# Scatters in batches of four that wait for landings, in place of waits on PE's progress

## What is computed

```python
x = x + (segment_sum(edge_weight * h[dst], src) @ weight + bias)
x = x + ((1 + eps) * h + segment_sum(relu(h[src] + edge_attr), dst))
x = x + L2(h)   # twice: segment_sum(w * x[c], r), w = dinv[r] * dinv[c], with self loops
x = x + L3(h)   # segment_sum(h[row] * norm, col), with self loops
```

## Time and profile before

| | us |
|---|---|
| median of 3 runs | 9,079.17 (9,056.56 to 9,087.81) |
| the profiled execution | 9,074.16 |
| its span | 9,072.3 |
| PE busy | 6,311.8 (70%) |
| DVE busy | 5,135.0 (57%) |
| ACT busy | 3,658.8 (40%) |
| POOL busy | 4,155.1 (46%) |
| POOL's scatters, 3,125 | 3,071.8, 983 ns each |

### The profile page before, as it was taken

One profiled execution on the slowest core, in us unless ns is written; L12 is line 12 of the kernel. 1 busy time (PEld: TensorE's weight loads), 2 busy tenths in 40 slices (PEclk: granted clock), 3 DMA queues, 4 the chain that ended last, 5 costly groups with the idle time before them and its releaser, 6 DMA issues.

```text
span 9072.3 us, 246452 instructions
## 1 busy us (share of the span) xinstructions
PE 6311.8 (70%) x98024; PEld 5439.8 (60%) x98025; DVE 5135.0 (57%) x7430; ACT 3658.8 (40%) x6626; POOL 4155.1 (46%) x4228
## 2 busy tenths in 40 slices
PE   5555555555555555555555555579999899999999
PEld 4444444444444444444444444468888899999999
DVE  5555555555555555555555555599999911111565
ACT  3444444444444444444444444478888600000000
POOL 2455555555555555555555555568888600000000
PEclk6677666676666667666666676799999999999999
DMA  6666566666666666666665666579999987888998
GB/s 172 186 180 179 177 181 183 183 187 179 190 183 181 177 179 200 182 177 181 191 185 177 185 190 184 162 251 316 316 318 316 306 272 261 283 276 277 283 266 213
DMA packets 1540180, 1969.31 MB, mean 217 GB/s; under 512 B 620045, under 2 KB 1204095, under 8 KB 1538767
## 3 DMA queue, kind: packets, MB, share of 16 engines
q1 hardware_dynamic: 1064800, 1272.38, 47.4%
q10 hardware_dynamic: 374342, 523.47, 18.5%
q0 software_dynamic: 100000, 158.60, 5.6%
HBM read 1335.36 MB, written 618.65 MB: 215 GB/s over the span
## 4 chain that ended last, share of the span: by engine, by line
PE 41%; another core or an unknown queue 17%; issue 13%; DVE 12%; ACT 10%; ACTq 2%; DMA 2%; POOL 2%; SPq 0%; DVEq 0%; POOLq 0%
PE pG L2347 9%; PE pT L2230 7%; PE pG L2374 7%; ACT stg L2585 5%; PE pT L2234 3%; PE pG L2186 3%; DVE doh L1724 2%; PE pT L2347 2%; ACT dfar L2552 2%; PE pR L2347 2%; DVE msum L1936 2%; PE pG L2197 2%; PE pG L2195 1%; PE pG L2311 1%
## 5 line engine op out<-in xcount | busy, mean ns | idle before, releaser
L1420 POOL DMA_INDIRECT recB<-rec,qpos x3125 | 3071.8, 983 | 2782.7 <-PE pT L2230 1376.0
L2230 PE MATMUL pT<-soh,doh 128*128 128x128 bf16 x10600 | 1820.9, 269 | 1608.3 <-ACT stg L2585 1317.4
L2585 ACT CAST stg<-pT 128x512 fp8e4<-128x512 f32 x2650 | 1497.7, 585 | 1977.5 <-PE pT L2230 1147.4
L2230 PEld LDWEIGHTS pT<-soh,doh 128*128 128x128 bf16 x10600 | 1042.5, 118 | 1867.8 <-ACT stg L2585 1421.5
L2234 PE MATMUL pT<-car,qidb 128*128 128x256 fp8e4 x2597 | 932.9, 359 | 32.5 <-issue 32.0
L1732 DVE TENSOR_REDUCE val<-pG 128x5 f32<-128x490 f32 x628 | 417.6, 665 | 878.7 <-PE pG L2197 385.4
L1737 DVE TENSOR_TENSOR rec<-pG,wN 128x480 f32<-128x480 f32 x314 | 206.6, 658 | 1173.2 <-remote 1053.1
L2311 PE MATMUL pG<-mpl,doh 128*128 128x144 bf16 x10388 | 765.9, 227 | 38.6 <-POOL mpl L1471 28.7
L1724 DVE TENSOR_TENSOR doh<-dm,pG 128x2560 bf16<-128x2560 bf16 x530 | 783.7, 1479 | 3.0 <-ACT dm L2671 2.6
L1724 DVE TENSOR_TENSOR doh<-smd,pG 128x2560 bf16<-128x2560 bf16 x530 | 783.4, 1478 | 0.0
L1724 DVE TENSOR_TENSOR soh<-smd,pG 128x1280 bf16<-128x1280 bf16 x530 | 432.5, 816 | 514.9 <-PE pT L2230 376.8
(11 more groups left out here) (265 smaller groups left out, 14180.2 us busy)
## 6 DMA issues: line engine op xcount, KB each, us to landing
recB<-zt ACTq DMA_DIRECT2D x102, 2425.5 KB
brec<-recB SPq DMA_DIRECT2D x477, 495.0 KB
erec<-recB SPq DMA_DIRECT2D x477, 495.0 KB, 5.5
cl<-cA SPq DMA_DIRECT2D x80, 2560.0 KB, 10.9
cA<-stg ACTq DMA_DIRECT2D x530, 320.0 KB
cl<-cA SPq DMA_DIRECT2D x40, 2720.0 KB, 11.2
drow<-dlD SPq DMA_DIRECT2D x157, 640.0 KB
srowB<-srD SPq DMA_DIRECT2D x265, 320.0 KB, 5.9
```

The lines of the kernel that those rows point to most:

```text
L1420: p.indirect_dma_start(recF, bass.IndirectOffsetOnAxis(ap=qpos[:, s, c:c + 1], axis=0), rec[:, s, c, :], None).then_inc(s_sc[s], 16)
L2230: ins = t.matmul(bank[:, h * 256 + b * 128:h * 256 + b * 128 + 128], doh[:, o, 2 * e + b, h * 128:(h + 1) * 128], soh[:, o, 2 * e + b, :], ...
L2585: a.copy(stg[:, o, :, e * 256:(e + 1) * 256], B8[6 + (g * 5 + e) % 2][:, :].rearrange("p (h x) -> p h x", h=2), saturate=False).then_inc(e ...
```

## The change

The waits of `paced` and `ranked` are left out. The 20 scatters of a slot are five batches of four, counted through over all slots (`batches`); batch B raises semaphore B % 3, in place of one semaphore for each s, and begins when batch B-2 has landed. The five scatters of slot (0, 2) are batch 0. `slot_free` and the wait of the first `load_bucket` of a chunk wait for the three last batches of the slot in question (`all_landed`). `hold` with a value that is known when the program is built no longer raises its counter; nearly all holds of the first stage are of that kind.

```diff
@@ -229,7 +229,10 @@
 
         def hold(eng, sem_, val):
 
-            eng.wait_ge(sem_, val).then_inc(s_hold, 1)
+            if isinstance(val, int):
+                eng.wait_ge(sem_, val)
+            else:
+                eng.wait_ge(sem_, val).then_inc(s_hold, 1)
 
         def cols(ap, i, g):
             return ap[:, bass.ds(i * TL + g * G, G)]
@@ -1334,14 +1337,29 @@
 
             return K * 16 + (16 if s == 2 else 0)
 
-        def scattered(K, s):
-            return K * (16 * SB) + (80 if s == 2 else 0)
+        BATCH = 4
+
+        def batch_done(B):
+
+            return s_sc[B % 3], (B // 3 + 1) * 16 * BATCH + (16 if B % 3 == 0 else 0)
+
+        def batches(K, s):
+
+            return 1 + (mcnt(K, s) - 1) * (SB // BATCH)
+
+        def all_landed(eng, K, s):
+
+            if mcnt(K, s) == 0:
+                hold(eng, *batch_done(0))
+                return
+            for B in range(batches(K, s) + 2, batches(K, s) + 5):
+                hold(eng, *batch_done(B))
 
         def slot_free(eng, K, s):
 
-            if isinstance(K, int) and scattered(K - 1, s) <= 0:
+            if mcnt(K - 1, s) < 0:
                 return
-            hold(eng, s_sc[s], scattered(K - 1, s))
+            all_landed(eng, K - 1, s)
 
         def reached(eng, sem_, val):
             if not isinstance(val, int) or val > 0:
@@ -1387,21 +1405,7 @@
             io(p.iota(mio[:, :, :, :], [[SB, 3], [1, SB], [0, 2]], base=0, channel_multiplier=0,
                       allow_small_or_imprecise_dtypes=True))
 
-            PACE = {0: {2: 4, 4: 6, 6: 8, 8: 10, 12: 12, 14: 14, 16: 15, 18: 16},
-                    1: {2: 4, 4: 7, 6: 9, 8: 10, 10: 13, 12: 14, 14: 15, 18: 18},
-                    2: {2: 8, 4: 10, 6: 13, 8: 14, 10: 15, 16: 16, 18: 19}}
-            RANKED = {0: {13: 2, 17: 3}, 1: {9: 1, 13: 3, 17: 4}, 2: {11: 1, 14: 2}}
-
-            def paced(K, s, c):
-
-                back, g = SUMMED[s][1]
-                hold(p, e_ca, ((K - back) * JG + g) * 5 + PACE[s][c])
-
-            def ranked(K, s, c):
-
-                hold(p, e_rk, (mcnt(K, s) + 1) * 4 + RANKED[s][c])
-
-            def scatter(K, s, first=False, pace=False, following=True):
+            def scatter(K, s, first=False):
                 n = mcnt(K, s)
                 hold(p, e_pos, n + 1)
                 hold(p, e_mu, n * 2 + 2)
@@ -1413,19 +1417,18 @@
                     for h in range(2):
                         hold(p, s_pz[h], K * 16)
                 for c in range(15 if first else 0, SB):
-                    if pace and c in PACE[s]:
-                        paced(K, s, c)
-                    if pace and following and c in RANKED[s]:
-                        ranked(K, s, c)
+                    B = 0 if first else batches(K, s) + c // BATCH
+                    if c % BATCH == 0 and B >= 2:
+                        p.wait_ge(*batch_done(B - 2))
                     p.indirect_dma_start(recF, bass.IndirectOffsetOnAxis(ap=qpos[:, s, c:c + 1], axis=0),
-                                         rec[:, s, c, :], None).then_inc(s_sc[s], 16)
+                                         rec[:, s, c, :], None).then_inc(batch_done(B)[0], 16)
 
             scatter(0, 2, True)
             for s in range(3):
                 scatter(1, s)
             for K in range(2, NK):
                 for s in range(3):
-                    scatter(K, s, pace=True, following=(K, s) != (NK - 1, 2))
+                    scatter(K, s)
             def aggregated(g):
 
                 p.wait_ge(e_ad, ((NK - 1) * JG + g) * 2 + 2)
@@ -2831,8 +2834,7 @@
             def load_bucket(K, g):
                 c = K * JG + g
                 if g == 0:
-                    for s in range(3):
-                        held(sp, s_sc[s], scattered(K, s))
+                    all_landed(sp, K, 2)
                 held(sp, e_ag, c - 4)
                 nb = nbk(g)
                 sp.dma_start(brec[:, g % 5, 0:nb, :], recB[bass.ds(K, 1), :, g * GB:g * GB + nb, :]
```

## The result

The changed kernel took 10,228.5 us (median of 4 runs, 10,209.4 to 10,239.4), the kernel before 9,083.5 beside it (4 runs, 9,056.6 to 9,093.1): a ratio of 1.126, 95% interval 1.123 to 1.129. Slower by 1,145 us; 10,800 had been forecast. The profiled execution took 10,209.4 us.

A forecast was written before the change was run, and what follows sets the result against it. Only the edge-sorting stage was taken to count: no engine full, a ring of waits with PE standing during POOL's unbroken scatters. 9,074 + 1,750 for longer slots - 20 for holds = 10,804, say 10,800 us; range 9,750 to 11,600.

The forecast's parts named there:

- PE stands in a run of scatters: Edge-sorting stage: PE stands while POOL scatters without pause, once a run is some 5 us old; chance 0.80, 10,800 us.
- POOL isn't the cause: Rival, first stage: PE stands for another reason, POOL's runs only fall beside it; 9,054 us, chance 0.08.
- The end of a stand: First stage: PE goes on shortly after POOL's last scatter, 0.35, 1.25 and about 3.3 us behind it in three cases.
- The list of 25.2 us: POOL in each slot: without paced waits, 20 scatters at 1.26 us run unbroken, 25.2 us.
- The waits on landings, taken as 0: POOL's new batch waits: mostly met before they are asked; one wait bounded by 0 and some 5 us, taken as 0.
- The price of a slot: Between positions of successive slots: 47.9 us against 36.4 before, 11.5 us more, times 152 = +1,750 us.
- the batches cut the runs: Rival, POOL's list: crowded landings pass 6.3 us and pause POOL; 9,930 us, or about 9,300; chance 0.07.
- The check by parts: Slot price from list, PE's restart and free flow: 49.4, 45.0 and 45.0 us, mean 46.5, +1,530 us.
- The holds, -20 us: ACT's holds before its 2,650 casts: without counters they merge with the next instruction; 20 us saved, bounds 0 and 45.
- SP's order at nothing: SP's load of a chunk's first bucket: released about 27 us after the positions instead of 36; nobody late for it.
- Slot-free waits at nothing: DVE, ACT and SP: three waits instead of one, some 5 us an engine, hidden in idle time; scatters long landed.
- the rival with 0.05: Rival, first stage: POOL's list sets the slot, so a list 10 us shorter gains 525 us: 8,550 us; chance 0.05.

The follow-up runs named there:

- e10: The changed kernel with a memset on POOL in place of each scatter, batch waits kept: 6,935 us beside 9,203 for the kernel before, ratio 0.753.
- e11: The kernel before without POOL's paced and ranked waits, nothing else changed, where PE posts late: 10,566 us, ratio 1.150 to the kernel before.
- e12: The changed kernel scattering 8 floats of each record instead of 99, where PE posts late: 10,370 us, ratio 1.129 to the kernel before.
- e5: The changed kernel itself run again, where PE doesn't post late: 7,688 us for 7,428 of the kernel before, ratio 1.035.
- e8: The kernel before without paced and ranked waits and with the edit of the holds, without the batches: 7,396 us for 7,421, ratio 0.997.
- e3: The kernel before with the edit of the holds alone: 7,403 us for 7,420 of the kernel before, ratio 0.998.
- e4: The changed kernel with batch B waiting for batch B-1 instead of B-2: 9,533 us for 7,420 of the kernel before, ratio 1.285.
- e2: The changed kernel with the paced and ranked waits put back: 7,757 us for 7,420 of the kernel before, ratio 1.045.
- e1: The kernel before without POOL's paced and ranked waits, where PE doesn't post late: 7,411 us, ratio 0.999 to the kernel before.

## Why the prediction was right, and where it wasn't

*PE stands in a run of scatters.* Right, for a late chip: the swap of the scatters for memsets (e10) takes every late post away, and without the pauses (e11) a late post is outstanding 42% of the time in place of 19%. The prediction's rival that POOL isn't the cause (9,054 us) is out.

The Trainium skill (SBUF — State Buffer, "SBUF: two separate sides" and "Who interferes with whom") says that transfers can't contend with a compute engine. The time that the prediction drew from it, 9,054 us, is refuted on a late chip, where PE did 1.73 us of matmuls in 19 us of scatters. The statement itself, on the ports, isn't tested by that: rows of a twelfth of the bytes made PE stand as long (e12), so what holds PE up need not be a transfer's access. On a prompt chip the traces agree with it (no late post in e5 or e8), and so they do for POOL's memsets on a late one.

*The end of a stand.* ACT's cast at 3029.84 comes 3.3 us behind the end of POOL's last scatter at 3026.57, as after slot (1,2).

*The list of 25.2 us.* Right: from 3001.59 to 3026.57, 25.0 us.

*The waits on landings, taken as 0.* This step failed in one slot of three. In 49 of the 51 middle slots of a chunk POOL waited for a landing, mostly at its 13th scatter:
```profile
2981.70 0.96 POOL L1423 DMA_INDIRECT recB<-rec,qpos  x1 [2.62 <-DMA recB<-rec,qpos]
...
3001.59 0.96 POOL L1423 DMA_INDIRECT recB<-rec,qpos  x1 [9.80 <-DVE qpos L1757]
```
Such a pause of 2.6 us ends the run, and PE gets through: from that slot's first scatter at 2964.08 to the next slot's at 3001.59 are 37.5 us. Over the execution middle slots with the pause took 40.0 us, the two without it 43.7, the first slots of a chunk 44.0, the last ones 47.7. In e11, where nothing cuts the runs, middle slots took 44.8, first ones 45.4 and last ones 49.2. That is the rival "the batches cut the runs", come true once in a chunk. It had a chance of 0.07 as a case by itself; as a term of the sum it would have had to stand with a number. The bound for a landing, 3.25 us, was read where DMA was quiet. The packets of the scatters' queue in the same trace of the kernel before hold later ones: the median scatter landed after 3.1 us, one in twenty after 7.7 or more. In the changed kernel the eighth scatter of a middle slot, for which the thirteenth waits, landed after 6.7 us, and POOL went on 1.8 us later (both medians), when the allowance is 6.3.

*The price of a slot.* This term was mis-sized: 47.9 us forecast, 43.9 measured, 11.5 over before forecast and 7.5 measured. As far as the runs show, the 4.0 us have three parts. The one slot from which the price was read: in e11, with runs that nothing cuts, slot (1,2) took 51.1 us, the last slots of a chunk 49.2 on average and all slots 46.5, 1.4 under the forecast. (Slot (1,2) took 50.8 us in the kernel before, 49.4 in e12 and 46.3 in the changed kernel itself, so one slot says it to a few us only.) The cut slots, (43.7 - 40.0)/3 = 1.2 us; the 43.7 are two slots, but e11's 44.8 say the same. The other 1.4 us stay unexplained; e11 ran in a sitting in which the kernel before took 98 us more, which would be 0.6 us a slot. The check by parts (46.5 us, +1,530) came closer, and its agreement with e11 is in part luck: it is slot (1,2) once more, without the 1.3 us from the positions to the first scatter, where the changed kernel has 0.5 (3001.13 to 3001.59).

*The runs before.* The prediction has them mostly of 4 to 8 scatters; by the trace 265 runs have four, 194 six, eight or ten, and 161 only two. Nothing in the sum uses it.

*The holds, -20 us.* -16 us on a prompt chip (e3); on a late one not measured alone. *SP's order at nothing:* not refuted. Its waits for the scatters fell from 1,042 us in 1000:5500 to 2.4, and the slot grew all the same. *Slot-free waits at nothing:* not refuted. One group names them,
```profile
DVE rec L1740 <- DMA recB<-rec,qpos: 558.1, 34, 18.4
```
but these wait for scatters three slots back, some 130 us old where 99% land within 7 us, and behind the same waits stands PE's post for the same instruction. The three semaphores now serve all slots, so some later scatter's landing on them is always near. One of them, of 17.8 us (2841.9 to 2859.7), lies beside a slot's scatters (2830.5 to 2857.7). *The last stages unchanged:* right, the windows above.

*The signs.* Runs of 20 with 0.30 us between came in two slots of three, and so did one long idle time in a slot, no landing among the longest waits, the clock (0.64 where about 0.6 was said) and the DMA rate (152 GB/s for 140); positions 46 to 51 us apart came for the last slots of a chunk alone.

*What the prediction couldn't see.* All its rows are from a late chip, and nothing in them says that another chip wouldn't stand. That the result came from a late one as well was luck. On a prompt one the forecast would have been wrong in size and in mechanism: +3.5%, from the landings (priced at 0), with POOL's list as what sets the slot, which was the rival with 0.05. That rival's own gain didn't come either, since on such a chip the paced waits hold next to nothing up (98 us in e3). The sign is the same on both.

Taken together, the change swaps pauses tied to PE's progress, which cost 0.1% on a prompt chip and keep 15% on a late one, for waits that give back about 2% on a late chip (1.129 for 1.150) and cost 3.8% on a prompt one (1.035 over 0.997). No kernel here is shown to beat the kernel before on both kinds: e8 is 0.3% quicker on prompt chips, but its scatters run without pauses like e11's, at 1.150 on late ones; e3, with the holds alone, is 0.2% quicker on prompt chips and wasn't run on a late one.

What stays open: what makes a chip late (chip number 7 came up with both kinds, at different times); which part of issuing or landing a scatter PE's posts wait behind; whether pauses of POOL's own (e4's) or the old waits beside the batches (e2's) would hold on a late chip. These weren't run there.

One sign in the traces points at the semaphores, and no run followed it up. On late chips only 17% to 36% of the scatters' additions to their semaphores are recorded singly, on prompt ones 96% or more in all nine experiments, though every wait on them is met. In e10, with no scatters, all 5,716 of PE's posts are recorded. Whether the additions are merged, or records of them are lost, the traces don't say. All executions on record carry a span and a granted clock, so some recording went on in each of them, and none says whether the recording has a part in the late posts.

## What to carry to other kernels

A wait that looks idle, because what it waits for needn't be done, may pace an engine whose work hurts another one; before it goes, look in the trace for a stretch that already lacks it, and read more than one such stretch, since the one slot was 4 us of 48 away from what came. A wait on a transfer's landing is free only while its allowance passes the slowest landing of the loop, not the usual one: here 6.4 us against a median of 3.8 and 8 at the end of a chunk's first slot, and 2.5 more until the waiting engine goes on. And run both kernels in more than one sitting, on more than one chip, before a reason is built on one.

## What the runs showed of the hardware

On some chips, or at some times, PE posts its semaphores late while GpSimd issues indirect scatters of 128 rows every 1.26 us: 20% to 24% of the recorded posts come over 1 us late, by up to 8 us in the kernel before and 12 to 14 us in those without its pauses. The slot is 36.4 us there even with the pauses; on a prompt chip it is 25.8 without them (e1), and the pauses cost 0.1%. In the changed kernel a late post is outstanding for 0 to 4% of the time in each of the first three microseconds of a run, 11% to 22% in the fourth to seventh, 62% in the eighth and 72% to 88% in the ninth to twelfth; after a run for 67% in the first two, 56% in the third, 19% in the fourth and none from the fifth on. It doesn't depend on the rows' bytes (396 or 32 each), memsets on the same engine don't cause it, and ACT's and the DVE's posts aren't touched. In other sittings the same kernels show none of it, at 7,420 us for 9,080 to 9,200.

An indirect scatter lands 1.8 us after its issue at the least, by its packets; on a prompt chip the median is 3.8 us and 95% land within 8.0 (e5). The engine that waits goes on 1.8 us (changed kernel) to 2.5 us (e5) after the last packet.

A late chip doesn't hold the granted clock down by itself: it was 0.69 in the first stage of the kernel before there, 0.85 with memsets in place of the scatters, and 0.81 on a prompt chip without pauses (e8).
